# Attention heads: PSUM banks per head, order of the maxima products, the division in pieces

## The chip, the cores and the metric

The kernel runs on one core of one Trainium2 chip. The metric is the device time of one execution in microseconds (us); lower is better. The kernel is one program of eight layers, and the change lies in one function of the fifth.

## The reference, cut to what matters

A residual stack of eight layers over one sequence of 2048 tokens of width 512. The fifth layer is a softmax attention with 16 heads of width 32, each token attending to all 2048:

```python
q = q * jnp.cos(rot)
k = k * jnp.sin(rot)
scores = jnp.einsum('bshd,bthd->bhst', q, k) / np.sqrt(dh).astype(np.float32)
scores = scores * spiral_weight[None, :, None, None]
attn = jax.nn.softmax(scores, axis=-1)
out = jnp.einsum('bhst,bthd->bshd', attn, v).reshape(b, s, d)
return out @ Wo.T + bo
```

## The kernel before

`attention` (L1138) runs four steps: `normalized_features`, `attention_inputs` (L1168: q, k, v, and the maxima of the first group of heads), `attention_heads` (L1333, the function that changes) and `project_and_add`. Between steps all engines meet at a barrier.

**Tiling.** The heads go in four groups of four (f = 0 to 3). Head h of a group has its 32 features on partitions 32h to 32h+31, so products with q or k use 32 rows of TensorE, another 32 for each head. A block is one group and 512 queries: 16 blocks. A block has 16 units, one for each tile of 128 keys; U counts all 256 units. `prob`, the exponentials of a unit (128 keys x 4 heads x 512 queries), has four buffers (NP = 4).

**A unit on TensorE**, groups 0 to 2 (L1501 to L1509), is two halves. The first half has `scores` of heads 0 and 1, `maxima` of heads 2 and 3, and half of the `values` of unit U-2 (256 queries); the second half has `scores` of heads 2 and 3, `maxima` of heads 0 and 1, and the other half of `values`. `scores` is a row product that puts minus the row maximum into a bank (L1444, bf16) and then the product k times q on top (L1447, f32). `maxima` (L1455) computes products q times k for the next group, of which only the maximum over each 512 keys is kept. `values` (L1468) adds prob times v into bank 7, four heads side by side on 32 columns each. An f32 product stands in the trace as two passes. In the first unit of a block `values` goes whole, at the unit's end. Group 3 (L1510 to L1513) has no maxima.

**Banks.** PSUM has eight. Score banks are 0, 1, 2 in turn; the row product of score n waits for the exponential of n-3 (L1425). Banks 3+4 and 5+6 are two pairs, used in turn by everything else: two maxima in one pair, or the sums, or the turned rows. `take` (L1414) waits until the use before last is read. In group 3 scores have banks 0 to 5, and other uses bank 6.

**Other engines.** ScalarE takes the exponential of each score (L1534), and copies bank 7 at the end of a block (L1540). Before unit U it waits until the users of prob of unit U-4 are done. VectorE reduces a pair of banks at a time (L1558); at the end of a block of maxima it splits the negated maxima into two bf16 parts (L1157, L1161, L1163). GpSimd sums the exponentials over the keys for the softmax denominator (L1410): 14 of 16 units are added in one accumulator, so 13 additions a block; in group 3 VectorE does them (L1595). TensorE adds up the rest (`sums`, L1481, in unit 17 of a block, that is the second of the next): 3 sources x 4 heads, with a matrix of ones. VectorE then takes the reciprocal of that bank, 512 columns at once (L1581), and multiplies (L1585). `turn_rows` (L1490) transposes the split maxima in the unit after `sums`, and VectorE copies them out (L1573).

## Time and profile before

| | us |
|---|---|
| median of 3 runs | 5199.88 (5199.38 to 5200.64) |
| the profiled execution's own time | 5199.14 |
| its span | 5197.4 |
| stage `attention_heads` (1233.8 to 2225.4) | 991.6 |
| in that stage busy: PE / DVE / ACT / POOL | 956.0 / 672.3 / 557.8 / 706.0 |

Busy time says little of a queue by itself: matmuls overlap, and PE counts as busy while any of them is in flight. The kernel is read by stage, and within this stage by block and by unit. PE is TensorE and PEld its weight loads, DVE VectorE, ACT ScalarE, POOL GpSimd. Consecutive records of one line are merged in the timeline: a row's second number is the time from the first start to the last end of its instructions.

### The profile page before, as it was taken

Reading aid. Unit: us, or ns where it says so; the run is one execution under the profiler, and the core shown is the slowest. Engines: PE = TensorE matmul, PEld = TensorE weight load, DVE = VectorE, ACT = ScalarE, POOL = GpSimd, SP = SyncE. Lnnn points to the kernel's source line nnn. Section 1 sums busy time; section 2 is a strip of 40 time slices with the busy share of each in tenths; the row PEclk is TensorE's granted clock in tenths of the full one; section 3 lists DMA queues with packets and bytes.
Section 4 is the critical chain, followed back from the end, with each engine's and each line's share of the span. In section 5 each row is a group of like instructions: output and inputs, shape, how many; then the busy total and the mean of one; then the engine's idle time right before and its main releaser. Section 6 shows DMA issues by size and latency. Waiting matters only on the chain. (4 is left out here: it accounts for less than half of the span.)

```text
span 5197.4 us, 65036 instructions
## 1 busy us (share of the span) xinstructions
PE 4674.0 (90%) x25716; PEld 2516.1 (48%) x25716; DVE 2376.8 (46%) x3173; ACT 1612.3 (31%) x2757; POOL 1663.4 (32%) x1050
## 2 busy tenths in 40 slices
PE   7359998899999999978999779999999989789996
PEld 3124443333333333246666446666665654466663
DVE  7865887366666666852222223333333331412222
ACT  5414442202555555822211122222222210222110
POOL 2010001003888887024555311111111110145553
PEclk9679999999999999988999889999999999889998
DMA  2000000100000000036888710000000022468887
GB/s 73 0 15 7 6 0 35 35 1 1 1 1 1 1 1 1 1 124 180 259 257 256 191 63 31 23 31 31 23 29 31 23 85 77 159 187 257 259 258 197
DMA packets 237579, 417.60 MB, mean 80 GB/s; under 512 B 31472, under 2 KB 119536, under 8 KB 237296
## 3 DMA queue, kind: packets, MB, share of 16 engines
q1 hardware_dynamic: 179952, 270.89, 15.5%
q0 software_dynamic: 57344, 142.64, 11.3%
q8 instruction: 213, 3.49, 0.3%
q14 instruction: 70, 0.57, 0.0%
HBM read 297.53 MB, written 115.93 MB: 80 GB/s over the span
## 5 line engine op out<-in xcount | busy, mean ns | idle before, releaser
L2363 PE MATMUL linb_pr_ps<-lin_z,linb_wt 128*128 128x512 f32 x1536 | 677.6, 594 | 17.0 <-POOL linb_slope_own L2333 17.0
L1534 ACT ACTIVATE attc_prob<-attc_ps 128x512 f32<-128x512 f32 x1024 | 549.0, 596 | 425.8 <-PE attc_ps L1447 376.6
L1410 POOL TENSOR_TENSOR attc_acc<-attc_acc,attc_prob 128x2048 f32<-128x2048 f32 x144 | 651.7, 4525 | 68.6 <-ACT attc_prob L1534 51.1
L1558 DVE TENSOR_REDUCE attc_peak<-attc_ps 128x2 f32<-128x1024 f32 x384 | 469.7, 1226 | 256.8 <-PE attc_ps L1455 256.8
L1447 PE MATMUL attc_ps<-att_q,att_k 32*128 32x512 f32 x2048 | 528.7, 612 | 0.0
L2363 PEld LDWEIGHTS linb_pr_ps<-lin_z,linb_wt 128*128 128x128 f32 x1536 | 286.2, 191 | 342.5 <-issue 324.5
L1455 PE MATMUL attc_ps<-att_k,att_q 32*128 32x512 f32 x1536 | 443.7, 654 | 2.9 <-DVE attc_tot L1581 2.9
L2340 POOL TENSOR_TENSOR linb_sq<-linb_osb 128x512 f32<-128x512 f32 x64 | 70.1, 1096 | 1039.4 <-ACT linb_osb L2466 1039.4
L2539 DVE SCALAR_TENSOR_TENSOR linb_gated<-linb_osb,linb_norm_w,linb_proj 128x512 f32<-128x512 f32 x64 | 94.4, 1475 | 668.0 <-ACT linb_osb L2466 668.0
L1468 PE MATMUL attc_ps<-attc_prob,att_v 128*32 128x256 f32 (+1 forms) x3472 | 318.2, 439 | 0.3 <-ACT attc_prob L1534 0.3
L1074 DVE TENSOR_TENSOR_SCAN ssmb_state<-ssmb_decay,ssmb_bu 128x2048 f32<-128x2048 f32 x64 | 280.8, 4413 | 54.3 <-PE ssmb_y_ps L927 29.4
L2048 POOL DMA_INDIRECT residual_rows<-moe2c_ye,moe2w_index x128 | 201.8, 1576 | 230.7 <-DVE moe2c_ye L2171 200.7
L2048 POOL DMA_INDIRECT residual_rows<-moe1c_ye,moe1w_index x128 | 201.6, 1575 | 230.2 <-DVE moe1c_ye L2171 200.8
L2449 ACT ACTIVATE linb_proj<-linb_pr_ps 128x512 f32<-128x512 f32 x192 | 114.7, 597 | 517.0 <-PE linb_pr_ps L2363 517.0
L1444 PE MATMUL attc_ps<-att_rows,attc_ones 32*128 32x512 bf16 x1024 | 248.4, 391 | 25.2 <-ACT attc_prob L1534 23.3
L927 PE MATMUL ssmb_y_ps<-ssmb_state,ssmb_diag 128*128 128x512 f32 x512 | 235.0, 606 | 19.5 <-DVE ssmb_y L1083 9.9
L2359 PE MATMUL linb_pr_ps<-linb_wt,lin_z 128*128 128x128 f32 x2048 | 233.8, 275 | 0.0
L2081 PE MATMUL moe2c_gu_ps<-moe2c_xt,moe2w_wgu 128*128 128x256 f32 x1024 | 233.6, 382 | 0.0
L2081 PE MATMUL moe1c_gu_ps<-moe1c_xt,moe1w_wgu 128*128 128x256 f32 x1024 | 233.5, 382 | 0.0
L2359 PEld LDWEIGHTS linb_pr_ps<-linb_wt,lin_z 128*128 128x128 f32 x2048 | 231.2, 192 | 0.5 <-issue 0.5
L783 POOL MEMSET ffn_nothing<- 128x512 f32 x2 | 1.1, 525 | 715.9 <-POOLq L61 715.9
L1468 PEld LDWEIGHTS attc_ps<-attc_prob,att_v 128*32 128x32 f32 x3472 | 68.6, 108 | 332.5 <-ACT attc_prob L1534 179.6
(439 smaller groups left out, 7482.7 us busy)
## 6 DMA issues: line engine op xcount, KB each, us to landing
moe1w_wgu<-in_L_ffn_gate_up_proj SPq DMA_DIRECT2D x32, 1536.0 KB
moe2w_wgu<-in_L_ffn_gate_up_proj SPq DMA_DIRECT2D x32, 1536.0 KB
moe1w_wd<-in_L_ffn_down_proj SPq DMA_DIRECT2D x32, 512.0 KB
gated_features<-linb_gated SPq DMA_DIRECT2D x64, 256.0 KB, 2.3
moe2w_wd<-in_L_ffn_down_proj SPq DMA_DIRECT2D x32, 512.0 KB
linc_gt<-gated_features SPq DMA_DIRECT2D x7, 2048.0 KB, 8.2
linb_wt<-in_L_attn_b_qkv_w SPq DMA_DIRECT2D x16, 768.0 KB, 4.6
residual_rows<-residual SPq DMA_DIRECT2D x8, 1024.0 KB, 4.3
```

Source lines behind the costliest of these rows:

```text
L1074: V.tensor_tensor_scan(state[:, s % RING, :], decay[:, s % RING, :], bu[:, e % 2, :], 0.0, ALU.mult, ALU.add).then_inc(state_done, 1)
L1410: pool.tensor_tensor(acc[:, n % 2, :, :], before, prob[:, U % NP, :, :], ALU.add).then_inc(pool_done, 2 if at == 1 else 1)
L1444: nc.tensor.matmul(ps[:, banks[-1], :], ones16[own, :], rows[own, cols], start=True, stop=False)
L1447: nc.tensor.matmul(ps[:, bank, :], k[own, f, keys], q[own, f, cols], start=False, stop=True).then_inc(s_done, 1)
L1455: last = nc.tensor.matmul(ps[:, bank + h % 2, :], q[own, f, i * P:(i + 1) * P], k[own, f, b * NB:(b + 1) * NB], start=True, stop=True)
L1468: last = nc.tensor.matmul(o_bank[h * DH:(h + 1) * DH, cols], v[:, i, at:at + DH], prob[:, U % NP, h, cols], start=(i == 0), stop=(i == TT ...
L1534: nc.scalar.activation(prob[:, U % NP, h, :], ps[:, n % 3 if at < 0 else at % 6, :], ACT.Exp).then_inc(exp_done, 1)
L1558: V.tensor_reduce(peak[:, w // TT % 2, i % QH, 2 * hp:2 * hp + 2, b], ps[:, bank:bank + 2, :], axis=AX.X, op=ALU.max).then_inc(mx_used, 1)
L2048: pool.indirect_dma_start(out=g.y_dram[x], out_offset=bass.IndirectOffsetOnAxis(ap=index[:, n // 2, n % 2:n % 2 + 1], axis=0), in_=ye[:, y ...
L2081: last = nc.tensor.matmul(gu_ps[:, x, part, :], wgu[:, j % PW, x, k, part * IN:part * IN + P], xt[:, j % 2, x, k, :], start=(k == 0), stop ...
L2359: last = nc.tensor.matmul(pr_ps[:, use % 2, c * CH:(c + 1) * CH], z[:, k, (t * TQ + c) * CH:(t * TQ + c + 1) * CH], wt[:, b, kind, k, :], ...
L2363: last = nc.tensor.matmul(pr_ps[:, use % 2, :], wt[:, b, kind, k, :], z[:, k, t * NB:(t + 1) * NB], start=(k == 0), stop=(k == DT - 1))
```

## The change

- Score banks are 0 to 3; a row product waits for the exponential of n-4.
- Banks 4, 5, 6 are single and used in turn. Each maxima product takes one and signals by itself; a use waits for the use three before it. VectorE reduces one bank at a time: four reductions of 512 columns in a unit, where there were two of 1024.
- In each half unit `maxima` comes before `scores`.
- ScalarE copies the summed bank into SBUF (`tot`, now two buffers) and frees it with a new semaphore `z_out`. VectorE takes the reciprocal in four pieces of 128 columns, one in each of four units, and then the four pieces of the multiplication in the next four.
- A block's additions go to two accumulators of seven units each (12 additions a block, three buffers in rotation), and `sums` has 4 sources, so 16 products.

```diff
@@ -1337,11 +1337,12 @@
         UNITS = TT * TC
         ALL = DT * UNITS
         NP = 4
+        HALF = 7
         SUMMED = (14, 15)
         POOLED = [i for i in range(TT) if i not in SUMMED]
         prob = L.sb("prob", [P, NP, QH, NB])
-        acc = L.sb("acc", [P, 2, QH, NB])
-        tot = L.sb("tot", [P, NB])
+        acc = L.sb("acc", [P, 3, QH, NB])
+        tot = L.sb("tot", [P, 2, NB])
         o_raw = L.sb("o_raw", [P, 2, NB])
         ones = L.sb("ones", [P, DH])
         ones16 = L.sb("ones16", [P, P], BF16)
@@ -1351,37 +1352,41 @@
...
-        vector_done = L.sem("vector_done")
+        vector_done, z_out, inverted = L.sem("vector_done"), L.sem("z_out"), L.sem("inverted")
...
         def uses_of(U):
             f, w = U // UNITS, U % UNITS
-            got = ["A", "B"] if f < DT - 1 else []
-            if U >= LAG:
-                done = (U - LAG) % TT
-                if done == TT - 1:
-                    got.append("F")
-            if w % TT == 2 and ((f < DT - 1 and w > TT) or (f > 0 and w == 2)):
-                got.append("R")
+            got = [("peak", h) for h in (2, 3, 0, 1)] if f < DT - 1 else []
+            if U >= LAG and (U - LAG) % TT == TT - 1:
+                got.append(("sums", 0))
+            if w % TT == 2 and ((f < DT - 1 and w > TT) or (0 < f < DT and w == 2)):
+                got.append(("rows", 0))
             return got
 
-        use_at, n_use = {}, 0
+        LAST_GROUP = (DT - 1) * UNITS
+        use_at, sums_upto, others_upto = {}, [0], [0]
         for U in range(ALL + LAG):
-            for kind in uses_of(U):
-                use_at[U, kind] = n_use
-                n_use += 1
-        LAST_GROUP = (DT - 1) * UNITS
-        USES_BEFORE = min(n for (U, kind), n in use_at.items() if U >= LAST_GROUP)
-
-        def use_banks(U, kind):
-            if U >= LAST_GROUP:
-                return 6
-            return 3 + 2 * (use_at[U, kind] % 2)
+            for use in uses_of(U):
+                use_at[U, use] = len(sums_upto) - 1
+                sums_upto.append(sums_upto[-1] + (use[0] == "sums"))
+                others_upto.append(others_upto[-1] + (use[0] != "sums"))
+        USES_BEFORE = min(n for (U, use), n in use_at.items() if U >= LAST_GROUP)
+
+        def use_bank(U, use):
+            return 6 if U >= LAST_GROUP else 4 + use_at[U, use] % 3
+
+        def use_count(U, use):
+
+            return others_upto[use_at[U, use] + 1]
 
         def rows_block(U):
             f, w = U // UNITS, U % UNITS
             return (f * TC + w // TT - 1) if w > TT else (f * TC - 1)
+
+        def accumulator(n, half):
+            return acc[:, (2 * n + half) % 3, :, :]
 
...
@@ -1398,37 +1403,40 @@
             pool.memset(ones16[:, :], 1.0).then_inc(ones_ready, 1)
             for n in range((DT - 1) * TC):
                 for at, i in enumerate(POOLED):
-                    if at == 0:
+                    if at % HALF == 0:
                         continue
                     U = n * TT + i
                     pool.wait_ge(exp_done, (U + 1) * QH)
                     if at == 1 and n >= 2:
                         pool.wait_ge(z_done, n - 1)
-                    if at >= 2:
+                    if at == HALF + 1 and n >= 1:
+                        pool.wait_ge(z_done, n)
+                    if at % HALF >= 2:
                         pool.wait_ge(pool_done, n * len(POOLED) + at)
-                    before = prob[:, (U - 1) % NP, :, :] if at == 1 else acc[:, n % 2, :, :]
-                    pool.tensor_tensor(acc[:, n % 2, :, :], before, prob[:, U % NP, :, :], ALU.add).then_inc(pool_done, 2 if at == 1 else 1)
+                    to = accumulator(n, at // HALF)
+                    before = prob[:, (U - 1) % NP, :, :] if at % HALF == 1 else to
+                    pool.tensor_tensor(to, before, prob[:, U % NP, :, :], ALU.add).then_inc(pool_done, 2 if at % HALF == 1 else 1)
 
         @block.tensor
         def _(pe):
-            def take(U, kind):
-                n = use_at[U, kind]
-                if U >= LAST_GROUP:
-                    pe.wait_ge(mx_used, n)
-                elif n >= 2:
-                    pe.wait_ge(mx_used, n - 1)
-                return use_banks(U, kind)
+            def take(U, use):
+                n = use_at[U, use]
+                before = n if U >= LAST_GROUP else max(n - 2, 0)
+                if others_upto[before]:
+                    pe.wait_ge(mx_used, others_upto[before])
+                if sums_upto[before]:
+                    pe.wait_ge(z_out, sums_upto[before])
+                return use_bank(U, use)
 
             def score_bank(n):
-                if n < QH * LAST_GROUP:
-                    if n >= 3:
-                        pe.wait_ge(exp_done, n - 2)
-                    return n % 3
                 at = n - QH * LAST_GROUP
-                if at < 3:
-                    pe.wait_ge(exp_done, n - 2)
-                elif at < 6:
-                    pe.wait_ge(mx_used, USES_BEFORE)
+                if at < 4:
+                    if n >= 4:
+                        pe.wait_ge(exp_done, n - 3)
+                    return n % 4
+                if at < 6:
+                    pe.wait_ge(mx_used, others_upto[USES_BEFORE])
+                    pe.wait_ge(z_out, sums_upto[USES_BEFORE])
                 else:
                     pe.wait_ge(exp_done, n - 5)
                 return at % 6
@@ -1446,15 +1454,14 @@
                     own = slice(h * DH, (h + 1) * DH)
                     nc.tensor.matmul(ps[:, bank, :], k[own, f, keys], q[own, f, cols], start=False, stop=True).then_inc(s_done, 1)
 
-            def maxima(U, kind, heads):
+            def maxima(U, heads):
                 f, w = U // UNITS + 1, U % UNITS
                 i, b = w // TC, w % TC
-                bank = take(U, kind)
                 for h in heads:
+                    bank = take(U, ("peak", h))
                     own = slice(h * DH, (h + 1) * DH)
-                    last = nc.tensor.matmul(ps[:, bank + h % 2, :], q[own, f, i * P:(i + 1) * P], k[own, f, b * NB:(b + 1) * NB],
-                                            start=True, stop=True)
-                last.then_inc(mx_done, 1)
+                    nc.tensor.matmul(ps[:, bank, :], q[own, f, i * P:(i + 1) * P], k[own, f, b * NB:(b + 1) * NB],
+                                     start=True, stop=True).then_inc(mx_done, 1)
 
             def values(U, half):
                 f, i = U // UNITS, U % TT
@@ -1470,12 +1477,12 @@
                 if half != 0:
                     last.then_inc(pv_done, 1)
 
-            def sums(U, kind):
+            def sums(U):
                 n = U - LAG
-                bank = take(U, kind)
+                bank = take(U, ("sums", 0))
                 sem, count = summed_by(n - n % TT + POOLED[-1])
...
-                sources = [prob[:, (n - 1) % NP, :, :], prob[:, n % NP, :, :], acc[:, n // TT % 2, :, :]]
+                sources = [prob[:, (n - 1) % NP, :, :], prob[:, n % NP, :, :], accumulator(n // TT, 0), accumulator(n // TT, 1)]
...
@@ -1499,22 +1506,22 @@
                     elif w == UNITS - TT:
                         pe.wait_ge(mx_step, f * TC)
                 if U < LAST_GROUP:
+                    maxima(U, (2, 3))
                     scores(U, (0, 1))
-                    maxima(U, "A", (2, 3))
                     if U >= LAG and (U - LAG) % TT:
                         values(U - LAG, 0)
+                    maxima(U, (0, 1))
                     scores(U, (2, 3))
-                    maxima(U, "B", (0, 1))
                     if U >= LAG:
                         values(U - LAG, 1 if (U - LAG) % TT else None)
                 else:
                     if U < ALL:
                         scores(U, range(QH))
                     values(U - LAG, None)
-                for kind in uses_of(U):
-                    if kind == "F":
-                        sums(U, kind)
-                    elif kind == "R":
+                for kind, _ in uses_of(U):
+                    if kind == "sums":
+                        sums(U)
+                    elif kind == "rows":
                         turn_rows(U)
...
@@ -1531,13 +1538,15 @@
                     n = QH * U + h
                     at = n - QH * LAST_GROUP
                     act.wait_ge(s_done, n + 1)
-                    nc.scalar.activation(prob[:, U % NP, h, :], ps[:, n % 3 if at < 0 else at % 6, :], ACT.Exp).then_inc(exp_done, 1)
+                    nc.scalar.activation(prob[:, U % NP, h, :], ps[:, n % 4 if at < 0 else at % 6, :], ACT.Exp).then_inc(exp_done, 1)
 
             def output(n):
                 act.wait_ge(pv_done, (n + 1) * TT)
                 if n >= 2:
-                    act.wait_ge(o_used, n - 1)
+                    act.wait_ge(o_used, QH * (n - 1))
                 nc.scalar.copy(o_raw[:, n % 2, :], o_bank).then_inc(o_out, 1)
+                act.wait_ge(z_done, n + 1)
+                nc.scalar.copy(tot[:, n % 2, :], ps[:, use_bank(n * TT + TT - 1 + LAG, ("sums", 0)), :]).then_inc(z_out, 1)
 
...
@@ -1549,70 +1558,69 @@
         def _(dve):
             V = nc.vector
 
-            def peaks(U, kind, hp):
+            def peak_of(U, h):
                 f, w = U // UNITS, U % UNITS
                 i, b = w // TC, w % TC
-                n = use_at[U, kind]
-                dve.wait_ge(mx_done, n + 1 - z_before[U, kind])
-                bank = use_banks(U, kind)
-                V.tensor_reduce(peak[:, w // TT % 2, i % QH, 2 * hp:2 * hp + 2, b], ps[:, bank:bank + 2, :],
+                dve.wait_ge(mx_done, use_count(U, ("peak", h)))
+                V.tensor_reduce(peak[:, w // TT % 2, i % QH, h, b:b + 1], ps[:, use_bank(U, ("peak", h)), :],
                                 axis=AX.X, op=ALU.max).then_inc(mx_used, 1)
...
-            def sums_out(U, kind):
-                n = (U - LAG) // TT
-                bank = use_banks(U, kind)
-                dve.wait_ge(z_done, n + 1)
-                V.reciprocal(tot[:, :], ps[:, bank, :]).then_inc(mx_used, 1)
-                dve.wait_ge(mx_used, use_at[U, "F"] + 1)
-                dve.wait_ge(o_out, n + 1)
+            def divide(n, step):
+
                 f, t = n // TC, n % TC
-                V.tensor_tensor(q[:, f, t * NB:(t + 1) * NB], o_raw[:, n % 2, :], tot[:, :], ALU.mult).then_inc(o_used, 1)
+                cols = slice(step % QH * P, (step % QH + 1) * P)
+                part = tot[:, n % 2, cols]
+                if step < QH:
+                    dve.wait_ge(z_out, n + 1)
+                    V.reciprocal(part, part).then_inc(inverted, 1)
+                else:
+                    dve.wait_ge(inverted, QH * n + step - QH + 1)
+                    dve.wait_ge(o_out, n + 1)
+                    V.tensor_tensor(q[:, f, t * NB:(t + 1) * NB][:, cols], o_raw[:, n % 2, cols], part, ALU.mult).then_inc(o_used, 1)
 
             def add(U):
                 n, at = U // TT, POOLED.index(U % TT)
                 dve.wait_ge(exp_done, (U + 1) * QH)
                 if at == 1:
                     dve.wait_ge(z_done, n - 1)
+                elif at == HALF + 1:
+                    dve.wait_ge(z_done, n)
                 else:
                     dve.wait_ge(vector_done, summed_by(U)[1] - 1)
-                before = prob[:, (U - 1) % NP, :, :] if at == 1 else acc[:, n % 2, :, :]
-                V.tensor_tensor(acc[:, n % 2, :, :], before, prob[:, U % NP, :, :], ALU.add).then_inc(vector_done, 2 if at == 1 else 1)
-
-            z_before, zs = {}, 0
-            for U in range(ALL + LAG):
-                for kind in uses_of(U):
-                    z_before[U, kind] = zs
-                    zs += kind == "F"
-            for U in range(ALL + LAG):
-                if LAST_GROUP <= U < ALL and U % TT in POOLED[1:]:
+                to = accumulator(n, at // HALF)
+                before = prob[:, (U - 1) % NP, :, :] if at % HALF == 1 else to
+                V.tensor_tensor(to, before, prob[:, U % NP, :, :], ALU.add).then_inc(vector_done, 2 if at % HALF == 1 else 1)
+
+            for U in range(ALL + LAG + 2 * QH):
+                if LAST_GROUP <= U < ALL and U % TT in POOLED and POOLED.index(U % TT) % HALF:
                     add(U)
-                for kind in uses_of(U):
-                    if kind == "A":
-                        peaks(U, "A", 1)
-                    elif kind == "B":
-                        peaks(U, "B", 0)
-                        if U % TT == TT - 1:
-                            split(U)
-                    elif kind == "R":
+                for kind, h in uses_of(U):
+                    if kind == "peak":
+                        peak_of(U, h)
+                    elif kind == "rows":
                         rows_out(U)
-                    else:
-                        sums_out(U, kind)
+                if U < LAST_GROUP and U % TT == TT - 1:
+                    split(U)
+                since = U - LAG - TT
+                if since >= 0 and since % TT < 2 * QH and since // TT < ALL // TT:
+                    divide(since // TT, since % TT)
```

## Rows read from the trace of the kernel before

**Rows 1.** Busy time by block; the window, us, busy by engine, PEclk, DMA share, GB/s.

```profile
1236.20:1302.90 66.70, 65.22 (x545) 22.15 (x544) 40.41 (x34) 34.75 (x64) 54.28 (x12) 0.88 0.00 1
...
1370.99:1439.06 68.07, 65.81 (x597) 22.41 (x596) 44.79 (x38) 35.22 (x66) 58.81 (x13) 0.97 0.00 1
...
1846.91:1913.79 66.88, 64.83 (x597) 22.13 (x596) 44.78 (x38) 35.22 (x66) 58.84 (x13) 1.00 0.01 1
...
2050.28:2095.16 44.88, 40.96 (x353) 11.60 (x356) 34.00 (x16) 33.53 (x65) 4.32 (x1) 1.00 0.00 1
2095.16:2135.73 40.57, 40.57 (x349) 11.45 (x352) 33.67 (x15) 33.52 (x65) 0.00 (x0) 1.00 0.00 1
```

**Rows 2.** Waits in the stage: who waited for whom, us in total, times, longest.

```profile
PEld attc_ps L1444 <- ACT attc_prob L1534: 98.7, 116, 1.8
...
ACT attc_prob L1534 <- POOL attc_acc L1410: 49.2, 34, 2.3
```

**Rows 3.** Timeline of one steady unit; start, us, engine, line, tiles, count, idle before.

```profile
1403.14 0.45 PE L1444 MATMUL attc_ps<-att_rows,attc_ones 32*128 32x512 bf16 x2
...
1403.22 0.70 PE L1455 MATMUL attc_ps<-att_k,att_q 32*128 32x512 f32 x2
...
1403.37 0.65 PE L1447 MATMUL attc_ps<-att_q,att_k 32*128 32x512 f32 x2
...
1404.38 0.64 PE L1468 MATMUL attc_ps<-attc_prob,att_v 128*32 128x256 f32 x8
...
1404.55 1.23 DVE L1558 TENSOR_REDUCE attc_peak<-attc_ps 128x2 f32<-128x1024 f32 x1 [0.58 <-PE attc_ps L1455]
...
1404.95 0.59 PE L1444 MATMUL attc_ps<-att_rows,attc_ones 32*128 32x512 bf16 x2
...
1406.33 0.64 PE L1468 MATMUL attc_ps<-attc_prob,att_v 128*32 128x256 f32 x8
...
1406.90 0.45 PE L1444 MATMUL attc_ps<-att_rows,attc_ones 32*128 32x512 bf16 x2
```

**Rows 4.** Timeline around the end of a block.

```profile
1377.94 1.90 PE L1481 MATMUL attc_ps<-attc_prob,attc_ones 128*32 128x512 f32 x16
...
1379.65 1.04 PE L1481 MATMUL attc_ps<-attc_acc,attc_ones 128*32 128x512 f32 x8
...
1380.63 0.39 PE L1444 MATMUL attc_ps<-att_rows,attc_ones 32*128 32x512 bf16 x2
...
1380.76 3.36 DVE L1581 RECIPROCAL attc_tot<-attc_ps 128x512 f32<-128x512 f32 x1 [1.89 <-PE attc_ps L1481]
...
1384.15 0.69 DVE L1585 TENSOR_TENSOR att_q<-attc_o_raw,attc_tot 128x512 f32<-128x512 f32 x1
1384.17 1.13 PE L1455 MATMUL attc_ps<-att_k,att_q 32*128 32x512 f32 x4 [0.29 <-DVE attc_tot L1581]
...
1387.10 0.61 PE L1490 MATMUL attc_ps<-ident,att_negp 128*128 128x128 bf16 x4
...
1387.64 0.61 PE L1444 MATMUL attc_ps<-att_rows,attc_ones 32*128 32x512 bf16 x2
```

**Rows 5.** Timeline of four maxima products in `attention_inputs`.

```profile
1069.46 1.14 PE L1243 MATMUL attb_mx_ps<-att_k,att_q 32*128 32x512 f32 x8
...
1070.64 2.36 DVE L1304 TENSOR_REDUCE attb_peak<-attb_mx_ps 128x2 f32<-128x1024 f32 x2 [2.75 <-PE attb_mx_ps L1243]
```

**Rows 6.** Instructions by line and shape: busy us, mean ns, idle before.

```profile
L1410 POOL TENSOR_TENSOR attc_acc<-attc_acc,attc_prob 128x2048 f32<-128x2048 f32 x144 | 651.7, 4525 | 68.6 <-ACT attc_prob L1534 51.1 <-POOL attc_acc L1410 0.4
...
L1558 DVE TENSOR_REDUCE attc_peak<-attc_ps 128x2 f32<-128x1024 f32 x384 | 469.7, 1226 | 256.8 <-PE attc_ps L1455 256.8
...
L1161 DVE CAST att_negp<-attc_neg 128x16 bf16<-128x16 f32 x12 | 11.5, 955 | 0.4
...
L1157 DVE TENSOR_REDUCE attc_neg<-attc_peak 128x16 f32<-128x64 f32 x12 | 2.6, 220 | 0.4
...
L123 DVE RECIPROCAL atta_norm_rstd<-atta_norm_dev 128x16 f32<-128x16 f32 x1 | 0.3, 252 | 0.3 <-ACT atta_norm_dev L128 0.3
```

11 lines of the change are left out of this document (6 added, 5 removed).

## The prediction

> **What bounds the kernel now.** I read the stage by blocks first, then the waits, then a steady unit instruction by instruction. A block takes 68.07 us, with TensorE in flight 65.81 of it; the other engines are busy 44.8 (DVE), 35.2 (ACT) and 58.8 (POOL) [rows 1]. So TensorE's queue sets the pace, and what matters is where it stands still. The timeline shows a unit of 3.76 us (row products at 1403.14 and, a unit later, 1406.90) made of two halves: 1.81 and 1.95 [rows 3]. Thirteen such units fill most of a block. In the first half the two row products span 0.45, where one alone takes 0.39 (the pair at 1380.63 starts together [rows 4]), so the second is 0.06 late; in the other half the span is 0.59, so it is 0.20 late [rows 3]. The second row product waits for an exponential, because three banks serve two scores a half; the waits list has 98.7 us of it, part of that hidden [rows 2]. The rest of a block, 68.07 - 16 x 3.76 = 7.9 us, is its end [rows 4]: `sums` 2.57 (8 records in (1379.65 - 1377.94) / 2 = 0.86, so 24 in 2.57); the unit behind it 7.01 where 3.76 is normal (1380.63 to 1387.64), since a maxima product stands behind the 3.36 reciprocal until 1384.17; and 2.1 left, mostly ScalarE waiting for POOL's additions (34 waits, 49.2 us, of which about half would be idle anyway [rows 2]). In most blocks the granted clock is also 0.97, a few us at the 1.2 GHz level after TensorE stood behind that reciprocal; a block granted 1.00 all through takes 66.88 [rows 1].
>
> **The change, part by part.**
>
> *Four score banks.* No row product waits for the half before it. From rows to values is 1404.38 - 1403.14 - 0.06 = 1.18, or 1406.33 - 1404.95 - 0.20 = 1.18; from values to the next rows 0.57 both times [rows 3]. A half without waits is 1.75; with two maxima issued ahead of it I take 1.76. That alone would give 3.52 a unit.
>
> *Three single maxima banks, maxima first.* This is the new wait. A half uses two banks, so its second maxima product needs the reduction of the first product of the half before. That ring is: product to start of reduction 1070.64 - 1069.46 = 1.18 [rows 5]; reduction of 512 columns; and 0.05 from the end of a VectorE instruction to a product that waits for it (1380.76 + 3.36 = 1384.12, then 1384.17 [rows 4]). The reduction: 1024 columns take 1.226 and 64 take 0.220 [rows 6], 1.05 ns a column, so 512 take 0.69; half of 1.226, 0.61, is the lower bound. The ring is 1.92 (1.84 to 1.92, and up to 2.07: maxima products take 1.14 from first start to last end [rows 5], which from 1403.22 is 1404.36, and the reduction starts at 1404.55 [rows 3]; if those 0.19 are VectorE's delay, and not the scores ahead in the program that must finish first, they belong in the ring). What stands behind this wait in TensorE's queue is everything: the row products, scores and values of the half. A half that waited is longer, so the next doesn't wait; two halves together cost 1.76 + 1.92 = 3.68 a unit, 0.08 less than now. I take 3.68 by the rows of products alone [rows 5]; bounds 3.60 and 3.83. The extra `z_out` wait ahead of each product has been met long before; no row shows its price, so it lies between 0 and the 0.05 of a met wait, at most 0.1 a unit. I take 0, as TensorE's queue is fed while values still run.
>
> The order matters too. In the trace the maxima pass starts at 1403.22, before the score pass at 1403.37 that is ahead of it in the program [rows 3]: on other rows of the array it needn't queue. So putting maxima first delays the scores by almost nothing. The Trainium skill (TensorE: Matmul & The Clock Gate, Step-by-step: what each phase is for) says that only weight loads are pulled ahead and "The MATMULs themselves stay in program order"; this case's rows differ. By that rule the move would cost what the fourth rival says.
>
> *DVE.* Four reductions are 2.8 a unit, up from 2.45: under 3.68. A reciprocal piece: 512 columns 3.36, 16 columns 0.25 [rows 4, 6], so 128 take 0.95. It comes after the unit's last reduction, and holds up the first reduction of the next by about 0.35, which passes through the ring to TensorE; the lengthened unit lets DVE catch up, so every other piece costs: 0.8 a block. A multiplication piece (a quarter of 0.69 [rows 4] plus overhead, 0.3) fits in the gap. The split of maxima (0.22 + 0.96 and a subtraction taken like the 0.22, with gaps 1.5 [rows 6]) was hidden behind the POOL wait; now it holds the ring up by 1.5 less DVE's slack of 0.6: 0.9 a block.
>
> *POOL.* Twelve additions of 4.53 [rows 6] are 54.3 a block, with a free unit in the middle. It falls behind 0.85 a unit, so 4.2 after six, then recovers; before it fell behind for thirteen. A unit's addition must end before the exponentials four units on start, some 12 us after its own end (4 x 3.7, less the 2.9 over which four exponentials are spread); with 4.5 for itself it ends 8.8 us after them in the first half of the block, 10.2 in the second, where it was 13. The wait is gone.
>
> *Sums.* Sixteen products, 3.43: 0.86 more, all on TensorE's path, so that unit is 3.68 + 3.43 = 7.11. ScalarE's copy (about 0.6) hides under the next scores. The unit behind it has no values in its first half: second maxima at 1.92 by the ring, +1.18 to values, +1.00 for whole values (0.57 + 0.43), +0.35 for the transposes (between a quarter and all of the 1387.64 - 1387.10 = 0.54 at the low clock [rows 4]): 4.45 instead of 7.01. With no stall of several us the low clock shouldn't come.
>
> *A block:* 14 x 3.68 + 7.11 + 4.45 + 0.9 + 0.8 = 64.8. The first three groups take 2050.28 - 1236.20 = 814.1 now [rows 1]; then 65.9 (the first block, 0.8 less) + 11 x 64.8 = 778.7: 35.4 less.
>
> *Group 3.* Its first block is 44.88, a middle one 40.57 [rows 1]: POOL's late additions and transposes behind a reciprocal. Of that excess about 4.0 goes. Four `sums` cost 0.86 more each: +3.4. DVE has room for the pieces (33.7 busy of 40.6, one addition a block less). The very last division is bare: 3.36 + 0.69 becomes a copy of 0.65, 4 x 0.95 and 4 x 0.3, +1.6. Sum +1.0.
>
> *Total* -34.4 from the profiled execution's 5199.14: 5164.7, say 5165. The median of the runs, 5199.88, is 0.7 above it, which I leave out.
>
> **The rivals.**
>
> 1. *The maxima ring takes back what the score banks give.* For it: 1404.55 is late after the product [rows 3], and three single banks are fewer than two pairs. Ring 2.07, unit 3.83: +0.15 x 14 x 12 = 25, so 5190. Against it: the first pair [rows 5] is reduced 1.18 after its start, with nothing ahead of it. A smaller dose, or a clock that still falls in the block's end (+1.2 x 10), gives 5177. Chance 0.20 for 5176 to 5196.
>
> 2. *Slower: one-bank reductions that are not much cheaper than the pair's.* All of TensorE's half stands behind them. It decides where a unit gains (68.07 - 64.8) / 14 = 0.23, that is a reduction of 0.92 in place of 0.69. At 1.0 the unit is 3.99: +0.31 x 14 x 12 = 52, so 5217; if it cost the whole 1.23, the unit would be 4.22 and DVE 4.9, far beyond. The met waits (0.1 a unit, 17 us) push the same way. Against it: the 0.22 for 64 columns [rows 6] leaves little fixed cost. Chance 0.09.
>
> 3. *More than forecast*: the low bound of the reduction (unit 3.60, -0.08 x 14 x 12 = -13) and pieces that collide with nothing (-0.8 x 12 = -10): 5142. Chance 0.05. That the units don't change at all and only the ends of blocks gain, so that four score banks don't do what they say, is 5165 + 13 = 5178 and lies in the first rival.
>
> 4. *Products keep program order.* Then the scores of a half start at least one pass (0.43) later: 0.86 a unit x 14 x 12 = +144, so 5309. The rows speak against it. Chance 0.02.
>
> **How the numbers follow.** My forecast has 0.64, its own range 5150 to 5176. About 0.2% (10.4 us) is what a measurement of this kernel can tell from no change: faster means below 5189.5. That is the forecast, the third rival and half of the first: 0.80; same 0.09; slower 0.11. The range leaves out the second and fourth rivals and the tail of the third: 5148 to 5196.
>
> **What would show each step.** Right: steady units of 3.6 to 3.75 with one half near 1.76 and one near 1.92; the one wait of a unit that of a maxima's weight load for a reduction; hardly any ScalarE wait for POOL; no wait behind the reciprocal; granted clock 1.00 from the second block on; reductions of 0.69. Wrong: reductions above 0.9, both halves waiting, or scores starting only after the second maxima pass.

## The result, and the profile after

The change made the kernel slightly slower. The median of 20 runs is 5208.52 us (5200.61 to 5213.45), against 5200.27 (5197.88 to 5202.97) for the kernel before: ratio 1.0015, 95% interval 1.0009 to 1.0021. The prediction was 5165, with 5148 to 5196 as its range. The profiled execution took 5213.45 us (span 5211.7), the longest of the 20.

Two lines of the page, the span and the busy times with their shares and instructions:

```profile
span 5211.7 us, 66496 instructions
...
PE 4692.4 (90%) x25844; PEld 2528.8 (49%) x25844; DVE 2459.7 (47%) x3649; ACT 1620.7 (31%) x2773; POOL 1607.3 (31%) x1038
```

By block (the view of [rows 1]; the blocks are cut at the first exponential of each):

```profile
1235.50:1295.31 59.81, 59.81 (x544) 22.93 (x543) 42.07 (x67) 34.74 (x65) 50.05 (x12) 0.95 0.00 1
1295.31:1370.18 74.87, 70.12 (x612) 24.10 (x604) 56.23 (x76) 35.80 (x66) 57.62 (x13) 0.93 0.00 1
1370.18:1439.07 68.89, 66.97 (x604) 23.53 (x604) 52.76 (x77) 35.81 (x67) 54.01 (x13) 0.98 0.01 1
1439.07:1509.87 70.80, 68.89 (x608) 23.96 (x604) 52.39 (x77) 35.80 (x66) 54.27 (x13) 0.95 0.00 1
...
2067.58:2109.16 41.58, 41.58 (x361) 11.81 (x364) 32.16 (x23) 34.11 (x67) 0.56 (x1) 1.00 0.01 2
2109.16:2150.60 41.44, 41.44 (x356) 11.68 (x360) 30.88 (x20) 34.10 (x66) 0.00 (x0) 1.00 0.00 1
```

The first block is 7.2 us shorter than before (66.70 [rows 1]; it begins at 1235.81). The eleven after it last 2067.58 - 1295.31 = 772.3, where before they lasted 2050.28 - 1302.90 = 747.4: 24.9 more. I had forecast 64.8 for each, and they average 70.2. Group 3 gives 3.3 back in its first block, and costs 0.9 (41.44 for 40.57) in the next and 0.6 (41.44 for 40.84) in the third. With the last block the whole stage is 18.3 longer; the rest of the program was 4.0 shorter in this execution.

What did come is in the waits (the view of [rows 2]):

```profile
PEld attc_ps L1463 <- DVE attc_peak L1565: 125.0, 209, 4.2
PEld attc_ps L1452 <- ACT attc_prob L1541: 46.6, 59, 0.8
PE attc_ps L1463 <- DVE attc_peak L1565: 24.3, 22, 3.3
ACT attc_prob L1541 <- POOL attc_acc L1418: 1.9, 2, 1.1
```

ScalarE's wait for GpSimd went from 49.2 us to 1.9. In its place TensorE waits for VectorE's reductions: 125.0 at the weight loads, part of it hidden, and 24.3 with nothing in flight. The maxima ring waits as forecast, once a unit, but "longest 4.2" is no ring of 1.92. The timeline shows both, in units 22 and 23 of one block (counted from its own exponentials, so 6 and 7 of the next). Rows of a steady unit, and then of the stall:

```profile
1465.79 0.39 PE L1452 MATMUL attc_ps<-att_rows,attc_ones 32*128 32x512 bf16 x2
...
1466.14 0.94 DVE L1592 RECIPROCAL attc_tot<-attc_tot 128x128 f32<-128x128 f32 x1
...
1467.69 0.39 PE L1452 MATMUL attc_ps<-att_rows,attc_ones 32*128 32x512 bf16 x2
...
1469.45 0.39 PE L1452 MATMUL attc_ps<-att_rows,attc_ones 32*128 32x512 bf16 x2
...
1469.90 3.14 DVE L1596 TENSOR_TENSOR att_q<-attc_o_raw,attc_tot 128x128 f32<-128x128 f32 x1
...
1471.20 1.12 PE L1463 MATMUL attc_ps<-att_k,att_q 32*128 32x512 f32 x2
1472.96 1.87 DVE L1565 TENSOR_REDUCE attc_peak<-attc_ps 128x1 f32<-128x512 f32 x3
1473.69 0.28 PEld L1463 LDWEIGHTS attc_ps<-att_k,att_q 32*128 32x128 f32 x1 [2.21 <-DVE attc_peak L1565]
1473.69 1.22 PE L1463 MATMUL attc_ps<-att_k,att_q 32*128 32x512 f32 x1 [1.38 <-DVE attc_peak L1565]
1473.70 0.61 PE L1452 MATMUL attc_ps<-att_rows,attc_ones 32*128 32x512 bf16 x2
```

The unit takes 1469.45 - 1465.79 = 3.66, in halves of 1.90 and 1.76, where before it took 3.76 [rows 3]. Behind its last reduction the first piece of the multiplication, 128 columns, lasts 3.14 us. The reductions behind it on VectorE start at 1472.96, the maxima product that waits for them at 1473.69, and every product of that half is queued behind it. After the stall the products run at the 1.2 GHz level (the row pair takes 0.61 instead of 0.39, and the granted clock reads 0.50 from 1474 to 1479).

GpSimd's records of the same stretch, in two views of the timeline (the second alone has only the later addition):

```profile
1468.37 9.17 POOL L1418 TENSOR_TENSOR attc_acc<-attc_acc,attc_prob 128x2048 f32<-128x2048 f32 x2
```

```profile
1473.03 4.51 POOL L1418 TENSOR_TENSOR attc_acc<-attc_acc,attc_prob 128x2048 f32<-128x2048 f32 x1
```

One addition runs from 1468.37 to 1472.89 (1468.37 + 4.52), and the multiplication ends 0.15 later, at 1473.04. All pieces, by line (duration in ns, shortest / median / longest):

```profile
L1596 DVE TENSOR_TENSOR att_q<-attc_o_raw,attc_tot x64: 228/1157/3169, 1331.7 to 2242.3; 128x128 f32<-128x128 f32 x64
```

```profile
L1592 DVE RECIPROCAL attc_tot<-attc_tot x64: 894/943/955, 1316.8 to 2240.9; 128x128 f32<-128x128 f32 x64
```

Of the 64 multiplications, 33 start while an addition runs. They take 1.15 to 3.17 us, and every one ends 0.15 after that addition. The other 31 take at most 0.29. Of the reciprocals 44 start inside an addition, and none is lengthened: many end well before it does.

The split of the maxima, at the end of a block, has the same trouble. VectorE's records at the end of the first block, GpSimd's, and the cast at the end of the next block:

```profile
1294.77 0.20 DVE L1161 CAST att_negp<-attc_neg 128x16 bf16<-128x16 f32 x1
1295.01 4.53 DVE L1163 TENSOR_TENSOR att_negp<-attc_neg,att_negp 128x16 bf16<-128x16 f32 x1
1299.42 1.87 DVE L1565 TENSOR_REDUCE attc_peak<-attc_ps 128x1 f32<-128x512 f32 x3
```

```profile
1290.29 9.17 POOL L1418 TENSOR_TENSOR attc_acc<-attc_acc,attc_prob 128x2048 f32<-128x2048 f32 x2
```

```profile
1369.36 1.70 DVE L1161 CAST att_negp<-attc_neg 128x16 bf16<-128x16 f32 x1
```

A subtraction of 16 columns takes 4.53, and ends 0.08 after the addition; that block's unit 16 takes 10.55. In the other blocks it is the cast of 16 columns that takes 1.69 to 2.00, and ends 0.06 after an addition; unit 16 is 4.9 to 5.2, once 7.05. I call a VectorE instruction that waits like this *held*.

### The profile page after: what moved, and what is told of

It reads as the page before. It is cut to its first block and busy times, and to the rows that moved or that the text cites. A ratio compares the mean times of both kernels' runs of the same rounds, so it can differ in the third digit from the quotient of the medians.

```text
span 5211.7 us, 66496 instructions
## 1 busy us (share of the span) xinstructions
PE 4692.4 (90%) x25844; PEld 2528.8 (49%) x25844; DVE 2459.7 (47%) x3649; ACT 1620.7 (31%) x2773; POOL 1607.3 (31%) x1038
## 3 DMA queue, kind: packets, MB, share of 16 engines
q8 instruction: 217, 3.56, 0.3%
## 5 line engine op out<-in xcount | busy, mean ns | idle before, releaser
L1565 DVE TENSOR_REDUCE attc_peak<-attc_ps 128x1 f32<-128x512 f32 x768 | 492.5, 683 | 197.7 <-PE attc_ps L1463 195.7
L1418 POOL TENSOR_TENSOR attc_acc<-attc_acc,attc_prob 128x2048 f32<-128x2048 f32 x120 | 542.6, 4522 | 44.3 <-ACT attc_prob L1541 30.4
L1463 PE MATMUL attc_ps<-att_k,att_q 32*128 32x512 f32 x1536 | 518.9, 660 | 25.9 <-DVE attc_peak L1565 24.3
L1455 PE MATMUL attc_ps<-att_q,att_k 32*128 32x512 f32 x2048 | 486.5, 613 | 0.0
L2547 DVE SCALAR_TENSOR_TENSOR linb_gated<-linb_osb,linb_norm_w,linb_proj 128x512 f32<-128x512 f32 x64 | 94.3, 1474 | 668.1 <-ACT linb_osb L2474 668.1
L1463 PEld LDWEIGHTS attc_ps<-att_k,att_q 32*128 32x128 f32 x1536 | 157.6, 189 | 227.3 <-DVE attc_peak L1565 125.0
L1475 PEld LDWEIGHTS attc_ps<-attc_prob,att_v 128*32 128x32 f32 x3472 | 69.1, 109 | 341.7 <-ACT attc_prob L1541 171.8
L2603 PE MATMUL linc_y_ps<-linc_wt,linc_gt 128*128 128x512 f32 x512 | 222.5, 598 | 0.0
```

The lines of the kernel that those rows point to most:

```text
L1418: pool.tensor_tensor(to, before, prob[:, U % NP, :, :], ALU.add).then_inc(pool_done, 2 if at % HALF == 1 else 1)
L1455: nc.tensor.matmul(ps[:, bank, :], k[own, f, keys], q[own, f, cols], start=False, stop=True).then_inc(s_done, 1)
L1463: nc.tensor.matmul(ps[:, bank, :], q[own, f, i * P:(i + 1) * P], k[own, f, b * NB:(b + 1) * NB], start=True, stop=True).then_inc(mx_done, 1)
L1475: last = nc.tensor.matmul(o_bank[h * DH:(h + 1) * DH, cols], v[:, i, at:at + DH], prob[:, U % NP, h, cols], start=(i == 0), stop=(i == TT ...
L1565: V.tensor_reduce(peak[:, w // TT % 2, i % QH, h, b:b + 1], ps[:, use_bank(U, ("peak", h)), :], axis=AX.X, op=ALU.max).then_inc(mx_used, 1)
```

## The experiments

A block's units are counted on past its end: 16 is the first of the next block, in which the split of the maxima is felt, 17 has `sums`, 18 the turned rows. Pieces of the reciprocal stand on VectorE behind the reductions of units 18 to 21, pieces of the multiplication behind those of units 22 to 25. They are felt a unit later, so my figures for the multiplication are the lengths of units 23 to 26, from one unit's first exponential to the next's. The expectations name the same four by the pieces, as 22 to 25. All ratios are to the kernel before, run on the same chip; its medians there lie between 5198.67 and 5201.51. "Block" is a typical one of groups 0 to 2, and "eleven blocks" is the time from the second block to the end of group 2 in the profiled execution.

| kernel | median, us | ratio (95%) | block | eleven blocks |
|---|---|---|---|---|
| before | 5200.27 | | 66.9 to 68.4 | 747.4 |
| after the change | 5208.52 | 1.0015 (1.0009 to 1.0021) | 68.6 to 71.1 | 772.3 |
| e1, no multiplications | 5184.87 | 0.996 (0.9946 to 0.9975) | 65.2 to 68.4 | 740.6 |
| e2, multiplications late | 5173.75 | 0.9945 (0.9929 to 0.9962) | 65.23 | 724.0 |
| e3, multiplication on GpSimd | 5193.30 | 0.9984 (0.9974 to 0.9993) | 66.5 to 68.9 | 750.4 |
| e5, scores first | 5241.71 | 1.0074 (1.0058 to 1.0091) | 70.5 to 73.5 | 791.0 |
| e4, e3 and split on GpSimd | 5142.85 | 0.9892 (0.9875 to 0.9908) | 63.17 | 695.3 |
| e7, additions of 4 columns | 5142.32 | 0.9889 (0.9872 to 0.9905) | 63.18 | 695.5 |
| e8, one multiplication | 5221.62 | 1.0042 (1.0028 to 1.0056) | 69.1 to 71.3 | 772.2 |
| e9, e2 and split on GpSimd | 5144.63 | 0.9893 (0.9877 to 0.991) | 63.15 | 695.2 |
| e6, e4 with scores first | 5152.47 | 0.9909 (0.9893 to 0.9926) | 64.07 | 705.0 |
| e12, e4 with one accumulator | 5156.21 | 0.9917 (0.9901 to 0.9934) | 64.2 | 706.7 |
| e10, before with split on GpSimd | 5199.72 | 1.0002 (0.9993 to 1.0012) | 68.1 | 747.1 |

The two columns don't always agree. Outside the stage the changed kernel's profiled execution is 4 us shorter than that of the kernel before and e1's 8 longer, with the others between, and no run here tells why; the changed kernel's profiled execution also lies 4.9 above its median. So a difference of medians can miss what happens in the stage by some 10 us; the last column shows the stage's own part.

### e1: the multiplications left out

```diff
...
-                else:
-                    dve.wait_ge(inverted, QH * n + step - QH + 1)
-                    dve.wait_ge(o_out, n + 1)
-                    V.tensor_tensor(q[:, f, t * NB:(t + 1) * NB][:, cols], o_raw[:, n % 2, cols], part, ALU.mult).then_inc(o_used, 1)
```

> The 64 multiplications of the division are left out (so the output isn't divided by the softmax sums); everything else is the changed kernel. Theory A (a VectorE instruction with two SBUF inputs waits until GpSimd's running addition has ended, and the maxima ring passes that wait to TensorE): the units 22 to 25 of a block fall from about 7.6 + 3.7 + 3.7 + 4.2 to 4 x 3.66, so 4.5 to 6 us a block in 11 blocks, 50 to 65 us: 5143 to 5158. Rival B (VectorE is merely overloaded by four more instructions of 0.28 each): 1.1 us a block, 12 us: 5196. Rival C (the long units come from the reciprocal pieces or the ring itself): no change, 5208.

Measured 5184.87 (5164.75 to 5192.15 over 7 runs). Units 23 to 26 are 3.66 each, so the stall there was the multiplication's. But the gain is 24 us (32 in the eleven blocks) where 50 to 65 were expected, because the other held instruction got worse. Rows of the end of a block, and the windows of unit 16 and of unit 17 behind it:

```profile
1624.52 4.52 POOL L1418 TENSOR_TENSOR attc_acc<-attc_acc,attc_prob 128x2048 f32<-128x2048 f32 x1
...
1626.84 2.25 DVE L1161 CAST att_negp<-attc_neg 128x16 bf16<-128x16 f32 x1
...
1629.98 0.54 PE L1452 MATMUL attc_ps<-att_rows,attc_ones 32*128 32x512 bf16 x2
1630.31 1.06 PE L1455 MATMUL attc_ps<-att_q,att_k 32*128 32x512 f32 x2
```

```profile
1627.38:1635.60 8.22, 7.14 (x40) 2.10 (x36) 4.72 (x7) 2.17 (x4) 1.66 (x1) 0.67 0.00 0
1635.60:1643.20 7.60, 7.60 (x69) 2.67 (x66) 2.45 (x5) 3.23 (x6) 4.04 (x1) 0.91 0.01 2
```

Without the long multiplications TensorE runs ahead, GpSimd's additions stand later relative to the end of a block, and the cast waits 2.25 instead of 1.70. Behind it the granted clock falls (0.67 over unit 16) and a score pair takes 1.06 where 0.59 is normal. So unit 16 costs 8.2 in most blocks instead of 5.2. The theory was right on the multiplication, and wrong in taking the cast's 1.7 for fixed.

### e2: the same multiplications where GpSimd is idle

Two pieces in each of the first two units of the next block but one (units 32 and 33), where GpSimd has ended one block's additions and not begun the next's.

```diff
...
-                if since >= 0 and since % TT < 2 * QH and since // TT < ALL // TT:
-                    divide(since // TT, since % TT)
+                if since >= 0 and since // TT < ALL // TT:
+                    if since % TT < QH:
+                        divide(since // TT, since % TT)
+                    elif since % TT >= TT - 2:
+                        for step in (2 * (since % TT - TT + 2), 2 * (since % TT - TT + 2) + 1):
+                            divide(since // TT, QH + step)
```

> The same 64 multiplications, moved from the units 22 to 25 of a block to its units 32 and 33 (two in each), where GpSimd has no addition to do. Same instructions, same engine, same count. Theory A: they take 0.28 each and the gain is nearly that of leaving them out, 45 to 60 us: 5148 to 5163. Rival B (overload): the 0.28 are still on VectorE, 5205 to 5210. If a multiplication in unit 33 meets the first addition of the next block, it takes up to 4.5 us, but under the sums, at no cost.

Measured 5173.75, above the expected 5148 to 5163. The view of one block, and the multiplications by line:

```profile
1626.87:1692.10 65.23, 64.14 (x608) 22.82 (x604) 48.11 (x77) 35.83 (x66) 54.31 (x13) 1.00 0.01 1
```

```profile
L1596 DVE TENSOR_TENSOR att_q<-attc_o_raw,attc_tot x64: 228/284/4641, 1365.1 to 2195.2; 128x128 f32<-128x128 f32 x64
```

62 of the 64 pieces start outside an addition and take 0.23 to 0.29. The two that start inside one take 4.63 and 4.64, and end 0.15 after it. The same instructions on the same engine in another place are worth 35 us (5208.5 to 5173.8), and 48 in the eleven blocks; the theory had 45 to 60. The block still has the held cast (2.27 in most blocks, unit 16 5.73), and in three blocks the granted clock is at 0.50 behind it (unit 16 6.9 to 8.0).

### e3: the multiplication whole on GpSimd

Between its two accumulators GpSimd has a free unit; there it does the 512 columns at once.

```diff
+            def multiply(n):
+                f, t = n // TC, n % TC
+                pool.wait_ge(inverted, QH * (n + 1))
+                pool.wait_ge(o_out, n + 1)
+                pool.tensor_tensor(q[:, f, t * NB:(t + 1) * NB], o_raw[:, n % 2, :], tot[:, n % 2, :], ALU.mult).then_inc(o_used, QH)
...
                 for at, i in enumerate(POOLED):
+                    if at == HALF and n >= 1:
+                        multiply(n - 1)
...
-                    V.tensor_tensor(q[:, f, t * NB:(t + 1) * NB][:, cols], o_raw[:, n % 2, cols], part, ALU.mult).then_inc(o_used, 1)
```

> The multiplication is done by GpSimd itself, 512 columns at once, in the free unit between its two accumulators; VectorE keeps the reciprocal pieces. Theory A: no VectorE instruction with two SBUF inputs is left among the additions but the split of the maxima; GpSimd has 1.2 us more in a block where it has 4 or more to spare: 5145 to 5160. If GpSimd's time is tight (additions late, ScalarE waits for them), the gain is smaller, and the waits of the exponentials for GpSimd's additions show it.

Measured 5193.30, where 5145 to 5160 was expected. Again units 23 to 26 are 3.66, and again the split takes what is won:

```profile
L1161 DVE CAST att_negp<-attc_neg x12: 202/3471/3751, 1294.3 to 2044.2; 128x16 bf16<-128x16 f32 x12
```

With more work on GpSimd the last additions of a block come later still, and the cast waits 3.47. The missed expectations of e1 and e3 have one cause, and e4 removes it.

### e4: e3, with cast and subtraction on GpSimd too

```diff
-                split_maxima(V, dve, neg, left_step, negp, peak[:, w // TT % 2], n, neg_done)
+                V.tensor_reduce(neg[:, :], peak[:, w // TT % 2].rearrange("p i h b -> p (i h) b"), axis=AX.X, op=ALU.max, negate=True).then_inc(left_step, 1)
...
+                pool.wait_ge(left_step, 2 * n + 1)
...
+                pool.tensor_copy(parts[:, :, :, 0], negs).then_inc(left_step, 1)
+                pool.wait_ge(left_step, 2 * n + 2)
+                pool.tensor_tensor(parts[:, :, :, 1], negs, parts[:, :, :, 0], ALU.subtract).then_inc(neg_done, 1)
```

> As e3_mult_pool, and the cast and the subtraction that split the maxima also run on GpSimd, behind its last addition of the block. Theory A (VectorE waits for GpSimd's running addition in every instruction that uses SBUF twice, the cast of 16 columns too: 3.46 us in e3): the wait of 3.4 us in unit 15 goes, unit 16 falls from 8.5 to about 4 us, and with it the low clock behind it: about 45 us less than e3, 5143 to 5153. Rival (GpSimd is now too full, 1.2 us for the multiplication and the split behind its queue): TensorE waits for the turned rows or ScalarE for the additions, 5170 or more.

Measured 5142.85: faster than both kernels, by 57 us than the kernel before. One block, and GpSimd's records behind its last addition:

```profile
1486.12:1549.30 63.18, 63.18 (x608) 22.68 (x604) 44.95 (x71) 35.82 (x67) 55.98 (x16) 1.00 0.01 1
```

```profile
1488.95 0.26 POOL L1430 CAST att_negp<-attc_neg 128x16 bf16<-128x16 f32 x1
1489.29 0.27 POOL L1432 TENSOR_TENSOR att_negp<-attc_neg,att_negp 128x16 bf16<-128x16 f32 x1
```

TensorE is never without work in the block (63.18 of 63.18), the clock is granted in full, and unit 16 takes 3.66. The split is done at 1489.56, long before the turned rows need it.

### e7: VectorE untouched, GpSimd's additions short

This is the test by itself: all of VectorE's instructions stay as in the changed kernel, and only GpSimd's additions shrink. It leaves out part of the softmax denominator: in groups 0 to 2 the additions cover 4 of 512 query columns, and the rest of the accumulators holds ones.

```diff
...
+            pool.memset(acc[:, :, :, :], 1.0).then_inc(blank, 1)
+            pool.wait_ge(blank, 1)
...
-                    pool.tensor_tensor(to, before, prob[:, U % NP, :, :], ALU.add)
+                    pool.tensor_tensor(to[:, :, 0:4], before[:, :, 0:4], prob[:, U % NP, :, 0:4], ALU.add)
```

> The changed kernel with GpSimd's additions cut to 4 of 512 columns of each head (the rest of the accumulators stays at 1, so the softmax sums are incomplete); every VectorE instruction is where the change put it. Theory A: all multiplications take 0.28 and all casts 0.20, units 22 to 25 take 3.66 and unit 16 below 4: about 6.5 us a block less, 5135 to 5145. Rival B (VectorE overloaded, or the place of the pieces is wrong in itself): the units 22 to 25 stay above 4 and the time above 5190.

Measured 5142.32, the same as e4. One block, and the three kinds of instruction by line:

```profile
1486.96:1550.14 63.18, 63.18 (x608) 22.70 (x604) 46.04 (x77) 35.80 (x67) 2.64 (x12) 1.00 0.01 1
```

```profile
L1598 DVE TENSOR_TENSOR att_q<-attc_o_raw,attc_tot x64: 228/282/285, 1326.8 to 2167.6; 128x128 f32<-128x128 f32 x64
```

```profile
L1161 DVE CAST att_negp<-attc_neg x12: 201/202/203, 1296.9 to 1991.8; 128x16 bf16<-128x16 f32 x12
```

```profile
L1420 POOL TENSOR_TENSOR attc_acc<-attc_acc,attc_prob x120: 219/220/222, 1248.7 to 1984.4; 128x16 f32<-128x16 f32 x120
```

Every multiplication, cast and subtraction has its short length again, in its old place in the queue. So nothing in VectorE's own order was at fault; the time lay in GpSimd's additions running beside it. What the collisions cost the changed kernel is 5208.5 - 5142.3 = 66 us (77 in the eleven blocks). e7 alone also takes most of GpSimd's load away; e4 keeps every addition at its full length, moves only the instructions that were held, and has the same block (63.17), so it is the meeting that costs, and not the additions as such.

### e8: one multiplication of 512 columns

```diff
-                if since >= 0 and since % TT < 2 * QH and since // TT < ALL // TT:
+                if since >= 0 and since % TT < QH + 1 and since // TT < ALL // TT:
...
-                    V.tensor_tensor(q[:, f, t * NB:(t + 1) * NB][:, cols], o_raw[:, n % 2, cols], part, ALU.mult).then_inc(o_used, 1)
+                    V.tensor_tensor(q[:, f, t * NB:(t + 1) * NB], o_raw[:, n % 2, :], tot[:, n % 2, :], ALU.mult).then_inc(o_used, QH)
```

> The changed kernel with the multiplication whole (512 columns, once, in unit 22) in place of four pieces in units 22 to 25. Theory A: one meeting with an addition in place of up to three; the first costs as before (3.1 us and 0.4 for the longer instruction), the others go: 0.5 to 1.5 us a block less, 5193 to 5205. Rival B (it is the work that counts): the same work in one place, 5208 or more.

Measured 5221.62, slower than four pieces, where a gain had been expected.

```profile
L1596 DVE TENSOR_TENSOR att_q<-attc_o_raw,attc_tot x16: 677/3548/3561, 1326.8 to 2244.0; 128x512 f32<-128x512 f32 x16
```

Eleven of the sixteen are held and take 3.54 to 3.56, that is until 0.55 after the addition; alone it takes 0.68. The length held is set by the addition, hardly by the size: 128 columns took 3.15 in the same place. So the two other holds of a block are gone, as expected (units 24 to 26 are mostly 3.66). But unit 23 takes 8.0 for 7.6, and the additions moved against the end of the block once more: the cast now waits 2.1 to 2.56, and unit 16 takes mostly 5.3 to 5.7, and 7.15 to 7.59 in the three blocks in which the granted clock falls to 0.50 behind the cast. In sum the eleven blocks last as long as in the changed kernel (772.2 and 772.3): no gain, and no loss either. The 13 us between the medians lie elsewhere: 8.5 outside the stage, and 4.9 because the changed kernel's profiled execution lies above its median. The time alone would fit rival B; the lengths don't, nor does e7, where the whole work is done at no cost.

### e5: scores first again, the rest of the change kept

```diff
-                    maxima(U, (2, 3))
                     scores(U, (0, 1))
+                    maxima(U, (2, 3))
...
-                    maxima(U, (0, 1))
                     scores(U, (2, 3))
+                    maxima(U, (0, 1))
```

> Only the order inside a half unit is put back: scores before maxima; banks, accumulators and the division stay as in the changed kernel. My theory of the ring: with the scores ahead in the queue only the maxima wait for the reduction, up to 0.2 us of that hides under the scores, and a steady unit falls from 3.66 to between 3.52 and 3.60: 15 to 25 us less, 5183 to 5193, with the stalls of the multiplications still there. Rival (maxima first is what makes the ring short, since their reduction starts only when the scores ahead have finished): a unit of 3.75 to 3.85, 5225 to 5240.

Measured 5241.71. The row products of three successive halves:

```profile
1577.32 0.39 PE L1452 MATMUL attc_ps<-att_rows,attc_ones 32*128 32x512 bf16 x2
...
1579.30 0.39 PE L1452 MATMUL attc_ps<-att_rows,attc_ones 32*128 32x512 bf16 x2
...
1581.05 0.39 PE L1452 MATMUL attc_ps<-att_rows,attc_ones 32*128 32x512 bf16 x2
```

The unit is 1.98 + 1.75 = 3.73, longer than the 3.66 with maxima first; my own theory had said shorter (3.52 to 3.60) and falls. Its maxima products start at 1577.34 and are reduced from 1578.68 on, 1.34 later; in the changed kernel a pair from 1444.62 is reduced from 1445.78 on, 1.16 later. The 0.07 a unit is 12 of the 19 us that the eleven blocks lose (772.3 to 791.0). The other 7 are the holds, which the other timing puts elsewhere; of the 33 between the medians 14 lie outside the stage or in the changed kernel's long profiled execution. All multiplications by line:

```profile
L1596 DVE TENSOR_TENSOR att_q<-attc_o_raw,attc_tot x64: 229/2234/4585, 1330.8 to 2263.5; 128x128 f32<-128x128 f32 x64
```

44 pieces are held here, against 33, and units 23 to 25 take mostly 5.4, 4.7 and 6.5 to 10. The cast is held in the first block alone, and unit 16 is 3.6 to 3.9. To see the order's own price the holds had to go first, which is e6.

### e6: e4 with scores first

```diff
-                    maxima(U, (2, 3))
                     scores(U, (0, 1))
+                    maxima(U, (2, 3))
...
-                    maxima(U, (0, 1))
                     scores(U, (2, 3))
+                    maxima(U, (0, 1))
```

> As e4_split_pool, with scores before maxima in each half unit as before the change: the order alone, with no stall at GpSimd around it. From e5_scores_first (3.73 a steady unit against 3.66): 0.07 x 15 units x 12 blocks = 11 to 14 us more than e4 (5142.85), 5153 to 5158, since the reduction of a maxima product placed behind the scores starts later and the ring is longer. Rival (the order costs nothing once the stalls are gone, the 3.73 of e5 came from them): 5141 to 5145.

```profile
1490.30:1554.37 64.07, 64.07 (x608) 23.80 (x604) 44.91 (x70) 35.69 (x67) 55.97 (x16) 1.00 0.01 1
```

Measured 5152.47: the block takes 64.07 for 63.18, and putting maxima first is worth 9.6 us (5152.47 - 5142.85; 9.7 in the eleven blocks), a little less than the 11 to 14 expected.

### e9: e2 with the split on GpSimd

```diff
-                split_maxima(V, dve, neg, left_step, negp, peak[:, w // TT % 2], n, neg_done)
...
+                pool.tensor_copy(parts[:, :, :, 0], negs).then_inc(left_step, 1)
...
+                pool.tensor_tensor(parts[:, :, :, 1], negs, parts[:, :, :, 0], ALU.subtract).then_inc(neg_done, 1)
```

> As e2_mult_late, and the cast and the subtraction of the split maxima on GpSimd. Theory A: unit 16 falls from 5.73 to about 3.8 us and the low clock in some blocks goes: 20 to 28 us less than e2 (5173.75), 5146 to 5154, about 1% faster than the kernel before. If the rows then come too late for the transposes in unit 18, TensorE waits there and the gain is smaller.

```profile
1483.21:1546.36 63.15, 63.15 (x608) 22.67 (x604) 45.73 (x75) 35.84 (x67) 55.12 (x15) 1.00 0.01 1
```

Measured 5144.63, by another way to the same block as e4 and e7. From e2 it is the split alone that changed, and it gives 29 us, where 20 to 28 was expected. One piece of 64 was held (2.48).

### e12: e4 with one accumulator of 14 units

```diff
-        HALF = 7
+        HALF = 14
...
-                    if at == HALF and n >= 1:
+                    if at == 7 and n >= 1:
...
-                sources = [prob[:, (n - 1) % NP, :, :], prob[:, n % NP, :, :], accumulator(n // TT, 0), accumulator(n // TT, 1)]
+                sources = [prob[:, (n - 1) % NP, :, :], prob[:, n % NP, :, :], accumulator(n // TT, 0)]
```

> As e4_split_pool, with one accumulator of 14 units in place of two of seven (13 additions a block, sums of 12 products): the accumulators alone. The sums give back 0.86 x 16 = 14 us. At 3.66 a unit GpSimd falls behind 0.87 a unit over 12 additions, 10.4, and with the last one's own 4.5 and the multiplication's 1.2 it ends 16 us behind, where some 12 are free: 3 to 4.5 us of ScalarE waiting for it in a block, 36 to 54 us. Sum 5165 to 5183. Rival (the wait is absorbed elsewhere in the block and the cheaper sums win): below 5143.

```profile
1493.77:1557.98 64.21, 64.20 (x601) 23.06 (x597) 44.96 (x72) 35.40 (x66) 60.48 (x16) 1.00 0.01 1
```

```profile
ACT attc_prob L1557 <- POOL attc_acc L1426: 117.7, 51, 2.9
```

Measured 5156.21. With 13 additions a block GpSimd (busy 60.48 of 64.21) falls behind, units 13 to 16 take 4.6 to 4.7 while ScalarE waits for it (4.0 more in all). Of that 2.9 comes back in unit 17, which takes 4.15 instead of 7.09: `sums` has one source less, 0.86, and the rest of its length lies beside the wait. Two accumulators are worth 13 us, where 22 to 40 was expected.

### e10: the kernel before with the split on GpSimd

The same lines as in e9, in the kernel before:

```diff
-                split_maxima(V, dve, neg, left_step, negp, peak[:, w // TT % 2], n, neg_done)
...
+                pool.tensor_copy(parts[:, :, :, 0], negs).then_inc(left_step, 1)
...
+                pool.tensor_tensor(parts[:, :, :, 1], negs, parts[:, :, :, 0], ALU.subtract).then_inc(neg_done, 1)
```

> The kernel before with one edit: the cast and the subtraction of the split maxima on GpSimd, behind its last addition. Their wait for GpSimd (0.96 us for a cast that takes 0.20 alone) stood where ScalarE was waiting for GpSimd's additions in any case, so nothing or little: 5192 to 5201. Rival (each cast's wait was on the path there too): 0.8 us a block, 5190 or less.

```profile
1439.71:1507.81 68.10, 65.88 (x597) 22.41 (x596) 43.74 (x37) 35.21 (x65) 59.26 (x15) 0.97 0.01 1
```

Measured 5199.72, ratio 1.0002 (0.9993 to 1.0012): no change, as expected. In the kernel before the cast was held as well, but TensorE was waiting at that point for other things.

## Why the prediction was wrong

**The step that failed** is "A multiplication piece (a quarter of 0.69 [rows 4] plus overhead, 0.3) fits in the gap". Its own length, 0.28, is right, and the gap is there. But 33 of the 64 pieces stand beside a GpSimd addition and are held until it ends. In most blocks units 23 to 26 take 7.60 + 3.67 + 3.66 + 4.19 instead of 4 x 3.66, so 4.5 more, with the granted clock at 0.50 for some 3 us behind the first hold. In the one block where it stays at 1.00 it is 3.9 more, and in the three where it is at 0.50 for some 7 us about 6. The kernel before had a multiplication of 0.69 [rows 4], and I took its length from there without asking what GpSimd did at that time. It did nothing: in the kernel before all 16 multiplications start outside an addition. The change moved them to a place where GpSimd works nearly all the time: of a block's four pieces three are held, and the third in order falls into GpSimd's free unit and takes 0.28.

**The same error stood in the term for the split.** I took the cast as 0.96 long [rows 6], and so the split as 1.5 with 0.9 on the path. The trace of before had the same cast also in an earlier form, without additions beside it (by line, shortest / median / longest in ns):

```profile
L1161 DVE CAST att_negp<-attc_neg x12: 707/986/1133, 1301.9 to 2049.3; 128x16 bf16<-128x16 f32 x12
L1161 DVE CAST att_negp<-attb_neg x4: 202/202/202, 1053.2 to 1231.2; 128x16 bf16<-128x16 f32 x4
```

Five times as long for the same tile size: that was the sign, and one could read it before the change. All twelve of the upper form end 0.06 after an addition. In the changed kernel the cast takes 1.7, and 2.1 to 3.8 in e1, e3 and e8: it depends on where the additions stand, and is no constant.

The Trainium skill (SBUF — State Buffer, Who interferes with whom) states this rule: VectorE shares its second pair of SBUF ports with GpSimd; a VectorE instruction with two SBUF inputs contends with a GpSimd instruction that reads SBUF, and so does one in a two-port mode, which copies and casts can enter; the lock is exclusive, and whichever comes second waits for the other's whole instruction. It also says that a reduction, and an instruction with one SBUF input outside those modes, doesn't contend. This case agrees: multiplication 3.14 and subtraction 4.53 (two inputs), cast 1.70 to 3.75, reciprocal 0.94 and reduction 0.68 unchanged beside additions. The other direction shows too. In e3 and e4, where group 3's additions are VectorE's, GpSimd's multiplication of 512 columns takes 2.86 to 3.15 beside them and 1.26 alone. My prediction had not weighed that rule, though it speaks directly against this change.

**The other terms**, against what was measured:

- *Steady unit 3.68*: 3.66. The ring of 1.92 is 1.90: 1.16 from product to reduction, 0.69, 0.05. The first rival (ring 2.07, unit 3.83) and the second (a reduction above 0.92) fall. A reduction of 512 columns is 0.68.
- *Maxima first costs nothing*: right, and better than that. With scores first the unit is 3.73 (e6). The fourth rival, that products keep program order at 0.86 a unit, falls.
- *Sums 7.11 and the unit behind it 4.45*: 7.09 and 4.42.
- *Reciprocal pieces 0.95 each, 0.8 a block*: 0.94 each; units 19 to 22 are 3.98 + 3.66 + 3.76 + 3.66, so 0.4 a block.
- *POOL's wait gone*: 49.2 to 1.9. In e12 the one accumulator brings 117.7 back.
- *Group 3*: first block -3.3 where I had -4.0, then +0.9, +0.6 and +2.4: +0.6 in all, for +1.0.
- *The split 0.9 a block*: 1.5 in unit 16 (5.17 for 3.66) as the change has it, and nothing in e7, where its cast takes 0.20. The slack of 0.6 in this term has no row: 3.68 less four reductions of 0.69 leaves 0.92.
- *The low clock shouldn't come*: it does, behind the holds (blocks at 0.93 to 0.98). In the blocks without stalls (e4, e7, e9) it is 1.00, so the reasoning holds and its condition failed. In the first block it does leave earlier: that block is 59.5, where I had forecast 65.9.

The sum without the holds would have been better than I forecast: e4 and e7 have blocks of 63.17, 1.6 below my 64.8. That is 0.9 for the split, 0.4 for the reciprocals and 0.3 for the units. Over eleven blocks it is 18 us, with 6 more in the first block, and 5165 - 24 = 5141 is what they measured (5142.3, 5142.9). So the change's own idea is worth 57 us, and the holds cost 66. The rival that should have stood on the slower side was this one; none of mine had an instruction of VectorE lengthened by GpSimd. That the result lies near the kernel before is no sign of small terms: a gain of 57 and a loss of 66 nearly cancel. (The parts of the chance of faster, 0.64, 0.05 and half of 0.20, add up to 0.79 and not 0.80.)

Open: why the granted clock behind the first hold of a block is at 0.50 for some 3 us in seven blocks (unit 23 of 7.25 to 7.62), for some 7 in three (8.6), and not at all in one (6.04), though all these holds last 3.14 to 3.17. The changed kernel's 20 runs spread over 13 us, those of the kernel before over 5 and e4's four over 3; that this comes from the clock is likely but not shown.

## What to carry to other kernels

Before moving an instruction on VectorE, look what GpSimd does at its new place, and whether both go through SBUF with two inputs (or a copy or cast): its length there is not its length elsewhere. An instruction of the same shape with two mean durations in one trace, 0.20 and 0.96 here, tells of such a hold before anything is built. Where a hold is removed, follow the other engine's timing on to the next instruction that it can hold: fixing one of two gave 24, 35 or 15 us (e1, e2, e3), fixing both 66 (e4).

## What the runs showed of the hardware that was not expected

- The wait depends on the addition and not on the held instruction: 16 columns took up to 4.56 us (0.23 alone, e3), 128 columns 4.64 (0.28), 512 columns 3.56 (0.68).
- It ends at a fixed distance from the addition's end: 0.06 for a cast of 16 columns, 0.15 for a multiplication of 128 and 0.55 for one of 512, in all 33 and all 11 cases of the two multiplications. GpSimd's next addition doesn't wait for that end: where additions follow each other at once the gap is 0.14, whether something is held or not. But in e8, where the held multiplication still runs 0.41 into it, it takes 4.77 to 4.78 instead of 4.52, in all eleven cases.
- Tiny instructions between long additions can take half of a change's gain: twelve casts and subtractions of 16 columns were worth 29 us (e2 to e9), since VectorE's reductions and TensorE's whole queue stood behind each.
- With f32 products on different rows of the array, the order in the program still matters to who signals first: the reduction starts 1.16 after a maxima product that is ahead of the scores in the program, and 1.34 after one that is behind them, though both start at nearly the same time.
